# Cross-attention and quantised FFN on one core: SyncE's loads reordered and grouped, the exponential ahead of the rounding, one small POOL move at the end

## Chip, cores and metric

One Trainium2 chip, one core. The metric is the device time of one launch in microseconds, the median of several runs. Inputs and outputs are float32 in HBM (the FFN weights are int8).

## What is computed

```python
x = x + xattn(layernorm(x), ctx, ctx, W, bias, mask)      # x, ctx: 8 x 512 x 512, mask: 8 x 512 x 512
x = x + ffn(layernorm(x), weight_q, weight_scale, ffn_bias)

def xattn(q1, key, value, weights, bias, drop_mask):
    scores = einsum('bqd,bkd->bqk', q1, key) / 0.72
    attn = softmax(scores, axis=-1) * drop_mask
    o = einsum('bqk,bkd->bqd', attn, value) + bias
    return einsum('bqd,de->bqe', o, weights)

def ffn(x, weight_q, weight_scale, bias):
    x_scale = maximum(max(abs(x), axis=-1), 1e-6) / 127.0
    x_q = clip(round(x / x_scale), -128, 127)               # int8
    return (x_q @ weight_q.T) * x_scale * weight_scale + bias
```

## The kernel before

The 8 x 512 rows of `x` are 32 tiles of 128 rows, four to a batch. A step `d` works on several tiles at once, and each engine runs the same sequence of steps: four first steps (tiles 0 to 3), three passes of a loop of eight steps (tiles 4 to 27, `base` 4, 12 and 20, written out by Python), and the last steps (`TAIL`, tiles 28 to 31 and what is left). All engines have their order written out by hand and meet at semaphores.

In a step `d` of the loop:

- TensorE (PE) makes `scores(d)` (12 products), `attend(d - 2)` (12, into `ps_attn`), `feed_forward(d - 4)` (4) and `next_vw(d + 4)` (12: a context tile times the attention weights). `scores` and the others in float32 are sums of three products of high and low parts, so each operand is split in two by ACT (`_hi`) and DVE or POOL (`_lo`).
- VectorE (DVE) turns the next context tile (`turn_ctx(d + 4)`, `ct_raw`), finishes the factors of the quantisation (`gains(d - 3)`), finds the row maximum (`highest`, `neg_max`), turns the next rows (`turn_x(d + 1)`, `xt_raw`), multiplies by the mask (`masked`, `probs(d)`), adds the residual (`residual(d - 2)`, `x`), turns the probabilities that came back from DRAM (`turn_probs(d - 1)`, `pt_raw`, L1223), and makes the low parts, `pt_lo` last.
- ScalarE (ACT) does `split_next_ctx` (`ct_hi`, L878), `round_integers(d - 3)` (`x_round`, L958), `store_integers(d - 3)` (`x_int`, L970), `exponentials` (L981), `split_next_x` (`xt_hi`, L913), `add_up_x(d + 4)` (the row sum of `x_in`, L896, for the layernorm), `split_late_vw`, `centre`, `split_bounced_probs(d - 1)` (`pt_hi`, L1000), `add_up_x1_squares` (`ps_ct`, L1017), `add_up_squares`, `normalise(d + 3)`, and then issues two DMAs of its own: the store of the normalised rows, and the store of a finished output tile, for which it waits for POOL's `add_up(d - 4)`.
- GpSimd (POOL) makes the low parts `ct_lo` and `xt_lo`, adds the bias, works out `rstd` by a power (`inverse_deviation`, L1569 and L1572) when ACT's squares are there, and adds up the output (`out_tile`, L1526).
- SyncE (SP) computes nothing: it waits and issues DMAs, in the order of its `step`. The queue moves on only when a wait is over and a DMA is issued.

Two things are turned by way of DRAM. The normalised rows are stored by ACT and read back by SP in four DMAs, one for each block of 32 columns (`load_rows`, L488). The probabilities are stored by SP (`store_probs(d - 1)`, L526), and when the store has landed SP reads them back in four DMAs (`load_probs(d - 1)`, L535) into `p_blocks`, which lies in `wq_rows`. `turn_integers(d - 4)` (L543) is a DMA transpose of `x_int`.

SP's step before, in order: context pair (only when `d` is even: four DMAs, L479), `turn_integers(d - 4)`, `load_rows(d + 1)`, `store_probs(d - 1)`, `load_x(d + 4)` (L470), `load_mask(d + 2)` (L492), `load_probs(d - 1)`. `x_in` has eight places for tiles, `mask_in` four, `ctx_in` four. `add_up_x(d + 4)` of ACT's step `d` is the first to read the tile that SP loads in its own step `d`.

## Time and profile before

| | |
|---|---|
| time, median of 3 runs | 329.21 us (328.72 to 329.78) |
| the profiled execution's own time | 328.42 us |
| its span | 326.6 us |
| TensorE busy, granted clock | 311.9 us (95%), 0.998 |
| DVE, ACT, POOL busy | 261.0 us (80%), 240.6 us (74%), 259.3 us (79%) |
| DMA | 68.39 MB, 209 GB/s over the span |
| chain that ended last, by engine | SPq 24%, DMA 22%, POOL 15%, ACT 11%, issue 9%, PE 9%, DVE 7% |

The busy time of TensorE counts matmuls whose ends are modelled, and they overlap: one of 512 columns is shown with 0.39 us, and the next starts 0.23 us later. So a busy share near 100% says only that it seldom stood still, and the pace is read from starts. "SPq" and "ACTq" are the issuing of DMAs by SyncE and ScalarE. A time in brackets at the end of a row is how long the engine had been idle before it, and for whom.

### The profile page before, as it was taken

What the parts mean: (1) busy time and instruction counts of PE and PEld (TensorE: products, weight loads), DVE (VectorE), ACT (ScalarE), POOL (GpSimd) and SP (SyncE); (2) the same over time, 40 slices, a digit from 0 to 9 for tenths busy, and PEclk for the clock granted to TensorE, in tenths of its full rate; (3) what the DMA queues carried; (4) which work ended last, traced back from release to release, by engine and by line L of the source; (5) the groups of instructions that cost most, each with busy time, mean ns of one, the idle gap of its engine ahead of it and who ended that gap; (6) DMA issues with size and microseconds to landing.
All of it is one profiled execution on the core that took longest, in us unless ns stands there. A gap on an engine that the chain in (4) does not pass through costs nothing.

```text
span 326.6 us, 5339 instructions
## 1 busy us (share of the span) xinstructions
PE 311.9 (95%) x1418; PEld 239.5 (73%) x1418; DVE 261.0 (80%) x565; ACT 240.6 (74%) x494; POOL 259.3 (79%) x362
## 2 busy tenths in 40 slices
PE   8999989999999999899998999999999999999982
PEld 7888767777777678677776777767778676776671
DVE  2998765988886899688887888788888778879775
ACT  5467867887887788788876889788787878866440
POOL 3274587897999789799997989899898879858683
PEclk9999999999999999999999999999999999999999
DMA  7995985798968979997888969998897996451112
GB/s 215 264 228 186 200 216 192 220 219 249 247 202 261 238 228 194 271 229 232 259 243 228 265 200 238 243 251 237 244 243 201 234 241 192 147 159 49 50 63 98
DMA packets 88173, 68.39 MB, mean 209 GB/s; under 512 B 25040, under 2 KB 67792, under 8 KB 88144
## 3 DMA queue, kind: packets, MB, share of 16 engines
q1 hardware_dynamic: 80368, 53.90, 65.3%
q10 hardware_dynamic: 7776, 14.16, 12.0%
q8 instruction: 11, 0.18, 0.3%
q14 instruction: 18, 0.15, 0.2%
HBM read 41.16 MB, written 22.54 MB: 195 GB/s over the span
## 4 chain that ended last, share of the span: by engine, by line
SPq 24%; DMA 22%; POOL 15%; ACT 11%; issue 9%; PE 9%; DVE 7%; ACTq 1%; POOLq 0%; DVEq 0%
DMA prob_rows<-probs 10%; DMA wq_rows<-prob_rows 8%; SPq L488 8%; SPq L535 7%; POOL out_tile L1526 5%; SPq L543 5%; SPq L479 4%; ACT x_round L958 2%; ACT ps_ct L1017 2%; POOL rstd L1572 2%; DVE pt_raw L1223 2%; ACT ct_hi L878 2%; ACT x_int L970 2%; POOL x_in L1560 2%; DMA norm_rows<-x_norm 1%
## 5 line engine op out<-in xcount | busy, mean ns | idle before, releaser
L636 PE MATMUL ps_attn<-vw_hi,pt_hi 128*128 128x512 f32 x120 | 47.9, 399 | 3.6 <-DVE pt_lo L1123 3.6
L636 PE MATMUL ps_scores<-ct_hi,xt_hi 128*128 128x512 f32 x124 | 48.7, 393 | 1.1 <-POOL xt_lo L1541 1.0
L638 PE MATMUL ps_scores<-ct_hi,xt_lo 128*128 128x512 f32 x124 | 48.3, 389 | 0.0
L637 PE MATMUL ps_scores<-ct_lo,xt_hi 128*128 128x512 f32 x124 | 48.3, 389 | 0.0
L638 PE MATMUL ps_attn<-vw_hi,pt_lo 128*128 128x512 f32 x120 | 46.8, 390 | 0.0
L637 PE MATMUL ps_attn<-vw_lo,pt_hi 128*128 128x512 f32 x120 | 46.8, 390 | 0.0
L1248 DVE TENSOR_TENSOR probs<-ps_scores,mask_in 128x512 f32<-128x512 f32 x32 | 22.0, 687 | 26.7 <-ACT ps_scores L981 26.3
L878 ACT ACTIVATE ct_hi<-ct_raw 128x512 fp32r<-128x512 f32 x28 | 17.7, 632 | 33.1 <-POOL out_tile L1526 30.4
L1560 POOL TENSOR_TENSOR x_in<-x_in,bias_w 128x512 f32<-128x512 f32 x32 | 41.5, 1296 | 0.7 <-issue 0.7
L1541 POOL TENSOR_TENSOR xt_lo<-xt_raw,xt_hi 128x512 fp32r<-128x512 f32 x29 | 37.7, 1301 | 4.1 <-ACT xt_hi L913 4.1
L1526 POOL TENSOR_TENSOR out_tile<-ffn_out,x_plus 128x512 f32<-128x512 f32 x28 | 39.6, 1415 | 0.0
L1586 POOL TENSOR_TENSOR x_plus<-x,ffn_bias_wide 128x512 f32<-128x512 f32 x28 | 36.3, 1297 | 3.7
L1533 POOL TENSOR_TENSOR ct_lo<-ct_raw,ct_hi 128x512 fp32r<-128x512 f32 x28 | 36.7, 1309 | 2.8 <-ACT ct_hi L878 2.8
L1139 DVE STREAM_TRANSPOSE xt_raw<-x_blocks 128x512 f32<-128x512 f32 x30 | 33.1, 1103 | 1.1 <-DMA x_blocks<-norm_rows 1.1
L810 PE MATMUL ps_ffn<-wq_t,xq_t 128*128 128x512 bf16 x120 | 31.1, 382 | 0.8 <-ACT xq_t L952 0.7
L1139 DVE STREAM_TRANSPOSE ct_raw<-ctx_in 128x512 f32<-128x512 f32 x28 | 30.8, 1099 | 0.0
L636 PEld LDWEIGHTS ps_attn<-vw_hi,pt_hi 128*128 128x128 f32 x120 | 22.5, 188 | 11.0 <-DVE pt_lo L1123 6.5
L888 ACT ACTIVATE x_norm<-x_in,norm 128x512 f32<-128x512 f32 x32 | 25.7, 804 | 5.2 <-POOL norm L1508 5.2
L636 PEld LDWEIGHTS ps_scores<-ct_hi,xt_hi 128*128 128x128 f32 x124 | 23.3, 188 | 7.1 <-POOL xt_lo L1541 2.4
L958 ACT ACTIVATE x_round<-x_neg,round_magic,neg_gain 128x512 f32<-128x512 f32 x31 | 24.9, 803 | 3.7 <-DVE neg_gain L1277 3.7
L636 PE MATMUL ps_vw<-w_hi,ct_hi 128*128 128x512 f32 x64 | 27.3, 427 | 0.0
L638 PEld LDWEIGHTS ps_scores<-ct_hi,xt_lo 128*128 128x128 f32 x124 | 23.3, 188 | 4.9
(187 smaller groups left out, 820.8 us busy)
## 6 DMA issues: line engine op xcount, KB each, us to landing
x_in<-in_x_dram SPq DMA_DIRECT2D x32, 256.0 KB, 4.1
mask_in<-in_mask_BxSxS_fk_dram SPq DMA_DIRECT2D x32, 256.0 KB, 4.4
norm_rows<-x_norm ACTq DMA_DIRECT2D x30, 256.0 KB, 4.0
x_blocks<-norm_rows SPq DMA_DIRECT2D x120, 64.0 KB, 2.4
ctx_in<-in_ctx_dram SPq DMA_DIRECT2D x56, 128.0 KB, 3.9
prob_rows<-probs SPq DMA_DIRECT2D x24, 256.0 KB, 2.3
wq_rows<-prob_rows SPq DMA_DIRECT2D x96, 64.0 KB, 3.5
out_dram<-out_tile ACTq DMA_DIRECT2D x24, 256.0 KB, 4.3
```

The costliest lines, as they stand in the source:

```text
L488: sp.dma_start(blocks.rearrange("i (a c) -> i a c", a=QUADS), quads[:, :, b * P:(b + 1) * P]).then_inc(x_blocks_loaded[slot(n, 2)], 16)
L636: nc.tensor.matmul(bank_, lhs_hi(t), rhs_hi(t), start=(t == 0), stop=False)
L637: nc.tensor.matmul(bank_, lhs_hi(t), rhs_lo(t), start=False, stop=False)
L638: last = nc.tensor.matmul(bank_, lhs_lo(t), rhs_hi(t), start=False, stop=(t == NT - 1))
L810: last = nc.tensor.matmul(ffn_bank(base, n)[:, :], xq_t[:, slot(n, 2), t, :], wq_t[:, t, :], start=(t == 0), stop=(t == NT - 1))
L958: nc.scalar.activation(x1_round[:, slot(n, 2), :], x1_neg[:, slot(n, 2), :], ACT.Identity, bias=round_magic[:, 0:1], scale=col(neg_gain, n ...
L1139: nc.vector.transpose(into.rearrange("p t (a i) -> p t a i", a=QUADS), blocks.rearrange("p (a j t) -> p t a j", a=QUADS, t=NT)).then_inc(r ...
L1526: nc.gpsimd.tensor_tensor(out_tile[:, slot(n, 2), :], ffn_out[:, slot(n, 2), :], x1_plus_of(base, n), ALU.add).then_inc(out_ready, 1)
L1533: nc.gpsimd.tensor_tensor(ct_lo[:, batch_of(n), :, j * P:(j + 1) * P], ct_raw[:, slot(n, 2), :, :], ct_hi[:, batch_of(n), :, j * P:(j + 1) ...
L1541: nc.gpsimd.tensor_tensor(flat(xt_lo[:, slot(n, 2), :, :]), flat(xt_raw[:, slot(n, 2), :, :]), flat(xt_hi[:, slot(n, 2), :, :].bitcast(F32 ...
L1560: nc.gpsimd.tensor_tensor(x_in[:, slot(d, 8), :], x_in[:, slot(d, 8), :], bias_w[:, :], ALU.add).then_inc(x_plus_ready, 1)
L1586: nc.gpsimd.tensor_tensor(into, x1_of(base, n), ffn_bias_wide[:, :], ALU.add).then_inc(x1_plus_ready, 1)
```

## The change

It has four parts.

1. SP's step becomes: `turn_integers(d - 4)`, `store_probs(d - 1)`, `load_rows(d + 1)`, `load_probs(d - 1)`, then what is loaded ahead. The store and the reading back of the probabilities move ahead of the rows and of `x` and the mask.
2. `x` and mask are loaded two tiles by one DMA, in even steps only (`load_two`), and the waits on their semaphores are rewritten for it (`wait_x`, `wait_mask`). The context pair is loaded at the end of two steps instead of at the start of one: one block in the even step, three in the odd one (`load_half_pair`).
3. In ACT's middle steps `exponentials` moves ahead of `round_integers` and `store_integers`.
4. For the last tile POOL's `inverse_deviation` moves ahead of `add_ffn_bias(d - 2)` and `add_up(d - 4)`.

```diff
--- before.py
+++ after.py
@@ -134,6 +134,22 @@
     ring = len(sems)
     uses = (PHASE + n) // ring + 1
     eng.wait_ge(sems[slot(n, ring)], base * (16 // ring) + (16 * uses - PHASE * (16 // ring)))
+
+
+def wait_x(eng, sems, tile):
+
+    if tile < PER_BATCH:
+        eng.wait_ge(sems[tile], 16)
+    else:
+        eng.wait_ge(sems[(tile - tile % 2) % 8], 16 * (tile // 8 + 1))
+
+
+def wait_mask(eng, sems, tile):
+
+    if tile < 2:
+        eng.wait_ge(sems[tile], 16)
+    else:
+        eng.wait_ge(sems[(tile - tile % 2) % 4], 16 * (tile // 4 + 1))
 
 
 def wait_pair(eng, sems, base, n):
@@ -479,6 +495,17 @@
                     sp.dma_start(blocks.rearrange("i t (a c) -> i (t a) c", a=QUADS),
                                  rows[:, :, b * P:(b + 1) * P]).then_inc(loaded[k // 2], 16)
 
+            def load_half_pair(base, n, h):
+
+
+                wait_count(sp, ct_raw_ready, base, n - 4 + 2 - PER_BATCH)
+                k = slot(n, 4)
+                rows = ctx_flat[bass.ds((base + n) * P, 2 * P), :].rearrange("(a i) d -> i a d", i=BLOCK)
+                for b in range(h, 1 if h == 0 else QUADS):
+                    blocks = ctx_in[b * BLOCK:(b + 1) * BLOCK, k:k + 2, :]
+                    sp.dma_start(blocks.rearrange("i t (a c) -> i (t a) c", a=QUADS),
+                                 rows[:, :, b * P:(b + 1) * P]).then_inc(ctx_loaded[k // 2], 16)
+
             def load_rows(base, n, row):
 
                 quads = norm_rows[bass.ds(row, P), :].rearrange("(a i) d -> i a d", i=BLOCK)
@@ -487,6 +514,11 @@
                     blocks = x_blocks[b * BLOCK:(b + 1) * BLOCK, slot(n, 4), :]
                     sp.dma_start(blocks.rearrange("i (a c) -> i a c", a=QUADS),
                                  quads[:, :, b * P:(b + 1) * P]).then_inc(x_blocks_loaded[slot(n, 2)], 16)
+
+            def load_two(into, rows, row, k, loaded):
+
+                sp.dma_start(into[:, k:k + 2, :], rows[bass.ds(row, 2 * P), :].rearrange("(t p) d -> p t d", p=P)) \
+                    .then_inc(loaded[k], 16)
 
             def load_mask(tile, k):
                 sp.dma_start(mask_in[:, k, :], mask_rows[bass.ds(tile, P), :]).then_inc(mask_loaded[k], 16)
@@ -551,15 +583,11 @@
             def step(base, d, row):
 
                 bounced = in_loop(base)
-                n = d + 4
-                if n % 2 == 0 and exists(base, n) and not is_tile(base, n, PER_BATCH) \
-                        and not is_tile(base, n, PER_BATCH + 2):
-
-                    wait_count(sp, ct_raw_ready, base, n - 4 + 2 - PER_BATCH)
-                    load_blocks(ctx_in, ctx_flat, row + n * P, n, 2, ctx_loaded)
                 n = d - 4
                 if exists(base, n) and (in_loop(base) or base + n < BY_PE):
                     turn_integers(base, n)
+                if bounced:
+                    store_probs(base, d - 1, row + (d - 1) * P)
                 n = d + 1
                 if is_tile(base, n, BY_PE_ROWS):
 
@@ -568,17 +596,17 @@
                 if exists(base, n) and not is_tile(base, n, 1) and (not last_batch(base) or d == 0):
                     load_rows(base, n, row + n * P)
                 if bounced:
-                    store_probs(base, d - 1, row + (d - 1) * P)
+                    load_probs(base, d - 1, row + (d - 1) * P)
                 n = d + 4
-                if exists(base, n):
-
-                    wait_count(sp, x1_ready, base, n - 8 + 1)
-                    load_x(row + n * P, slot(n, 8))
+                if exists(base, n) and d % 2 == 0:
+
+                    wait_count(sp, x1_ready, base, n + 1 - 8 + 1)
+                    load_two(x_in, x_rows, row + n * P, slot(n, 8), x_loaded)
                 n = d + 2
-                if exists(base, n):
-
-                    wait_count(sp, probs_ready, base, n - 4 + 1)
-                    load_mask(row + n * P, slot(n, 4))
+                if exists(base, n) and d % 2 == 0:
+
+                    wait_count(sp, probs_ready, base, n + 1 - 4 + 1)
+                    load_two(mask_in, mask_rows, row + n * P, slot(n, 4), mask_loaded)
                 if is_tile(base, d, 1):
                     load_ffn_constants()
                     sp.wait_ge(wq_rows_ready, 1)
@@ -588,8 +616,10 @@
                 if is_tile(base, d, PER_BATCH - 1):
 
                     sp.wait_ge(wq_turned, 16 * NT)
-                if bounced:
-                    load_probs(base, d - 1, row + (d - 1) * P)
+
+                n = d + 6 - d % 2
+                if exists(base, n) and base + n >= 2 * PER_BATCH:
+                    load_half_pair(base, n, d % 2)
                 n = d - 5
                 if is_tile(base, n + 1, LAST):
                     store_out(base, n, row + n * P)
@@ -890,7 +920,7 @@
 
             def add_up_x(base, n):
 
-                wait_dma(act, x_loaded, base, n)
+                wait_x(act, x_loaded, base + n)
                 if is_tile(base, n, SUMS_FROM):
                     act.wait_ge(xt_lo_ready, BY_PE_ROWS)
                 nc.scalar.activation(ps_xt[:, :], x_in[:, slot(n, 8), :], ACT.Identity,
@@ -1019,10 +1049,10 @@
 
                 if is_middle(base, d):
                     split_next_ctx(d + 4)
+                    exponentials()
                     if in_loop(base):
                         round_integers(d - 3)
                         store_integers(d - 3)
-                    exponentials()
                     split_next_x()
                     add_up_x(base, d + 4)
                     if in_loop(base):
@@ -1161,7 +1191,7 @@
 
             def x_statistics(base, n):
 
-                wait_dma(dve, x_loaded, base, n)
+                wait_x(dve, x_loaded, base + n)
                 nc.vector.bn_stats(stats1[:, slot(n, 4), :], x_in[:, slot(n, 8), :]).then_inc(stats1_ready, 1)
                 wait_count(dve, stats1_ready, base, n + 1)
 
@@ -1239,7 +1269,7 @@
                 def masked():
 
                     wait_count(dve, exp_ready, base, d + 1)
-                    wait_dma(dve, mask_loaded, base, d)
+                    wait_mask(dve, mask_loaded, base + d)
                     into, exps, mask_tile = probs[:, slot(d, 2), :], ps_scores[:, :], mask_in[:, slot(d, 4), :]
                     if is_middle(base, d) and base + d < TAIL - 1:
                         into = into.rearrange("p (b t j) -> p t b j", b=QUADS, t=NT)
@@ -1552,7 +1582,7 @@
 
                 def add_bias():
 
-                    wait_dma(pool, x_loaded, base, d)
+                    wait_x(pool, x_loaded, base + d)
                     if is_tile(base, d, 0):
                         pool.wait_ge(bias_w_ready, 1)
 
@@ -1636,10 +1666,10 @@
                         add_up(d - 4)
                         add_ffn_bias(d - 2)
                     else:
+                        if is_tile(base, d - 1, LAST):
+                            inverse_deviation(d - 1)
                         add_ffn_bias(d - 2)
                         add_up(d - 4)
-                    if is_tile(base, d - 1, LAST):
-                        inverse_deviation(d - 1)
                     if is_tile(base, d - 1, LAST):
                         add_ffn_bias(d - 1)
                 if is_tile(base, d - 2, LAST):
```

What the SP queue holds in an odd and an even step of the loop (`x_blocks` are the normalised rows, `prob_rows` the stored probabilities, `wq_rows` the place into which they are read back). Before, an even step:

```order
L479 DMA ctx_in<-in_ctx_dram 32x8x128 x4
L543 DMA_TRANSPOSE xq_t<-x_int 128x4x128
L488 DMA x_blocks<-norm_rows 32x4x128 x4
L526 DMA prob_rows<-probs 128x512
L470 DMA x_in<-in_x_dram 128x512
L492 DMA mask_in<-in_mask_BxSxS_fk_dram 128x512
L535 DMA wq_rows<-prob_rows 32x4x128 x4
```

The odd step had the same rows without the first. Now, the last row of an odd step and then an even step:

```order
L506 DMA ctx_in<-in_ctx_dram 32x8x128 x3
L575 DMA_TRANSPOSE xq_t<-x_int 128x4x128
L558 DMA prob_rows<-probs 128x512
L515 DMA x_blocks<-norm_rows 32x4x128 x4
L567 DMA wq_rows<-prob_rows 32x4x128 x4
L520 DMA x_in<-in_x_dram 128x2x512
L520 DMA mask_in<-in_mask_BxSxS_fk_dram 128x2x512
L506 DMA ctx_in<-in_ctx_dram 32x8x128
```

The odd step now begins with the same four rows and ends with the three context loads. The even step had 16 DMAs and the odd one 12; now each has 13, and `x` and the mask have moved from ahead of `load_probs` to behind it.

ACT in a step of the loop, from the split of the context tile to the sum of `x`. Before:

```order
L878 ACTIVATE ct_hi<-ct_raw 128x4x128
L958 ACTIVATE x_round<-x_neg,round_magic,neg_gain 128x512
L970 ACTIVATE x_int<-x_round 128x512
L981 ACTIVATE ps_scores,prob_sum<-ps_scores,neg_max 128x512
L913 ACTIVATE xt_hi<-xt_raw 128x512
L896 ACTIVATE ps_xt,x_sum<-x_in 128x512
```

Now:

```order
L908 ACTIVATE ct_hi<-ct_raw 128x4x128
L1011 ACTIVATE ps_scores,prob_sum<-ps_scores,neg_max 128x512
L988 ACTIVATE x_round<-x_neg,round_magic,neg_gain 128x512
L1000 ACTIVATE x_int<-x_round 128x512
L943 ACTIVATE xt_hi<-xt_raw 128x512
L926 ACTIVATE ps_xt,x_sum<-x_in 128x512
```

The exponential is two places earlier; `x_int` is one place later, and the sum of `x` stays where it was.

## Rows read from the trace of the kernel before

**Rows 1.** Timeline, TensorE: first product of scores for tiles 4, 8, 9, 28, and a pause

```profile
51.74 0.50 PE L636 MATMUL ps_scores<-ct_hi,xt_hi 128*128 128x512 f32 x1
...
88.21 0.39 PE L636 MATMUL ps_scores<-ct_hi,xt_hi 128*128 128x512 f32 x1
...
97.29 0.39 PE L636 MATMUL ps_scores<-ct_hi,xt_hi 128*128 128x512 f32 x1
...
213.71 0.50 PE L636 MATMUL ps_attn<-vw_hi,pt_hi 128*128 128x512 f32 x1 [0.56 <-DVE pt_lo L1123]
...
277.15 0.39 PE L636 MATMUL ps_scores<-ct_hi,xt_hi 128*128 128x512 f32 x1
```

**Rows 2.** Waits: engine, line, waited for: us in total, times, longest

```profile
ACT ct_hi L878 <- POOL out_tile L1526: 30.4, 23, 1.4
DVE probs L1248 <- ACT ps_scores L981: 26.3, 27, 1.3
...
DVE pt_raw L1223 <- DMA wq_rows<-prob_rows: 10.5, 11, 1.7
```

**Rows 3.** Timeline, SP's queue in an even step (start, us, what)

```profile
199.08 1.19 SPq L543 DMA_TRANSPOSE xq_t<-x_int  x1
200.32 2.00 SPq L488 DMA_DIRECT2D x_blocks<-norm_rows  x4
202.36 0.43 SPq L526 DMA_DIRECT2D prob_rows<-probs  x1
202.84 0.43 SPq L470 DMA_DIRECT2D x_in<-in_x_dram  x1
...
205.04 2.06 SPq L535 DMA_DIRECT2D wq_rows<-prob_rows  x4
```

**Rows 4.** Timeline, ACT: two steps without a pause, then the step from 205.10

```profile
91.62 0.63 ACT L878 ACTIVATE ct_hi<-ct_raw 128x512 fp32r<-128x512 f32 x1 [1.31 <-POOL out_tile L1526]
...
100.56 0.63 ACT L878 ACTIVATE ct_hi<-ct_raw 128x512 fp32r<-128x512 f32 x1 [1.32 <-POOL out_tile L1526]
...
204.71 0.34 ACTq L1039 DMA_DIRECT2D out_dram<-out_tile  x1
205.10 0.63 ACT L878 ACTIVATE ct_hi<-ct_raw 128x512 fp32r<-128x512 f32 x1 [1.32 <-POOL out_tile L1526]
...
206.47 0.63 ACT L970 ACTIVATE x_int<-x_round 128x512 bf16<-128x512 f32 x1
207.01 0.64 ACT L981 ACTIVATE ps_scores<-ps_scores,neg_max 128x512 f32<-128x512 f32 x1
...
208.19 0.59 ACT L896 ACTIVATE ps_xt<-x_in 128x512 f32<-128x512 f32 x1
```

**Rows 5.** DMA issues of the span: x count, KB, median us to landing

```profile
x_in<-in_x_dram SPq DMA_DIRECT2D x32, 256.0 KB, 4.1
mask_in<-in_mask_BxSxS_fk_dram SPq DMA_DIRECT2D x32, 256.0 KB, 4.4
```

**Rows 6.** DMA issues at 193.48 (first row) and at 166.27 (second row)

```profile
mask_in<-in_mask_BxSxS_fk_dram SPq DMA_DIRECT2D x1, 256.0 KB, 3.0
...
mask_in<-in_mask_BxSxS_fk_dram SPq DMA_DIRECT2D x1, 256.0 KB, 5.6
```

**Rows 7.** Timeline, DVE: probabilities of tile 3

```profile
49.58 0.65 DVE L1248 TENSOR_TENSOR probs<-ps_scores,mask_in 128x512 f32<-128x512 f32 x1
```

**Rows 8.** Timeline, POOL and DVE at the end, from the last tile's mean

```profile
314.42 0.21 DVE L1304 BATCH_NORM_AGGREGATE meanvar<-last_stats 128x2 f32<-128x12 f32 x1
...
314.42 1.27 POOL L1586 TENSOR_TENSOR ctx_in<-x,ffn_bias_wide 128x512 f32<-128x512 f32 x1
...
315.42 0.69 DVE L1262 TENSOR_REDUCE abs_max<-x_neg 128x1 f32<-128x512 f32 x1 [0.25 <-ACT x_neg L1011]
...
317.15 0.55 POOL L1572 TENSOR_TENSOR rstd<-var_eps,minus_half 128x1 f32<-128x1 f32 x1
...
317.81 0.21 DVE L1269 TENSOR_SCALAR q_range<-abs_max,rstd 128x1 f32<-128x1 f32 x1 [1.70 <-POOL rstd L1572]
```

## Prediction

> **What bounds the kernel now.** I read the page first. TensorE is shown busy for 95% of the span (the table above), so the question is how far it is from its own pace. The timeline of TensorE gives that: from the first scores product of tile 8 to that of tile 9 it is 97.29 - 88.21 = 9.08 us, with nothing idle between. The 24 steps of the loop run from 51.74 to 277.15 [rows 1], 225.4 us; 24 at 9.08 would be 217.9. So the loop has **7.5 us** of pauses to give, and no more. One of them is the row at 213.71, where the product with the probabilities waited for `pt_lo` [rows 1].
>
> The waits say why. DVE sat 10.5 us in eleven waits, up to 1.7 us, for the probabilities to come back from DRAM (`wq_rows<-prob_rows`), and `pt_lo` is made from these [rows 2]. SP's queue shows why they are late: in an even step it issues a transpose, four row loads, the store, `x` and the mask, and only then, at 205.04, four loads of probabilities, 5.96 us after the step's first issue [rows 3]. A context pair of over 2 us more stands ahead of all that.
>
> A second cycle lies right under TensorE's. ACT waits 30.4 us in all for POOL's `out_tile` before `ct_hi` [rows 2], and `out_tile` waits for ACT's squares through `rstd`: squares, `rstd`, `out_tile`, the store on ACT's queue, `ct_hi`, and along ACT back to the squares. Where nothing disturbs it, `ct_hi` follows `ct_hi` after 100.56 - 91.62 = 8.94 us [rows 4]. Two steps make 17.88 us against TensorE's 18.16. So ACT has **0.28 us for two steps** to lose, and whatever it waits beyond that lengthens the loop as if TensorE waited.
>
> **The change part by part.** The sum is made against the profiled execution's own 328.42 us; the median of the runs is 0.79 us above it.
>
> (a) *Probabilities earlier.* I count from ACT's `ct_hi` of step d. `x_int` ends at 206.47 + 0.63 - 205.10 = 2.00, and the exponential that is now ahead of it adds 0.66 (0.64 and the gap): 2.66, and SP issues the transpose at about 2.72. From the starts there [rows 3]: transpose 1.24, store 0.48, row loads 2.04. The loads of the probabilities begin at 6.5; the store, issued at 3.96, has then had 2.5 us (its wait before, with x and mask issued behind it, ended at 205.04 - 202.36 = 2.7). The last is issued at about 8.1 and DVE needs them about 12 after the same `ct_hi`: its own next step is 8.94 on, and maximum, turn, mask and residual, some 3 us, lie ahead of `turn_probs` in it. The eleven waits should go: **-7.5 us**. Above nothing, at worst 0, if they are late for the transpose ahead of the store.
>
> (b) *Exponential first.* DVE's 26.3 us of waiting for it [rows 2] shrink, about 1 us a step. DVE isn't the bound, so by itself this is worth 0; it is cover for (a). Its price is that `x_int`, on which SP's step now hangs first, is 0.66 later. TensorE uses the integers a step later, behind 24 products of 0.23 us: 0.
>
> (c) *x in pairs, behind the probabilities.* This is the new wait. The loads of the probabilities take about 1.9 (2.06 in [rows 3]), so the pair is issued at 8.4. Its first tile is summed in the very next ACT step, at 208.19 - 205.10 = 3.09 after `ct_hi` [rows 4], which is 8.94 + 3.09 = 12.03. It may take **3.65 us** to land, and 3.93 before the 0.28 is used up. What it will take no row shows, since no DMA before was of 512 KB. Nearest rows: one tile of `x` takes 4.1 median, and the mask issued 0.47 behind it lands after 4.4 [rows 5], so 512 KB in two DMAs are there 4.9 after the first issue. Lower end: the mask at 193.48 with 3.0 + 0.47 = 3.5; upper end: the one at 166.27 with 5.6 + 0.47 = 6.1 [rows 6]. I take **4.4**, between 4.1 and 4.9, because in those rows a 256 KB store stood directly ahead, and now small loads do, but ACT's store of an output tile, which it issues 0.39 ahead of `ct_hi` [rows 4], so at 8.55 on this count, falls on the same moment, with the store of the rows just ahead of it. Twelve even steps load a pair: 12 x (4.4 - 3.93) = **+5.6 us**. Ends: 0 at 3.5, and +26 at 6.1 if that were every step, which no stretch of the trace supports. Behind the waiting sum on ACT stand `vw_hi`, `x_neg`, `pt_hi` and the squares, so POOL's `rstd`, `out_tile` and `ct_lo` wait with it, and TensorE for `ct_lo`.
>
> [...]
>
> (d) *First even step of the loop.* Here SP is held by the store of tile 3's probabilities, ready at 49.58 + 0.65 = 50.2 [rows 7], not by `x_int`. The pair goes out 0.48 + 2.04 + 1.9 later, at 54.7, about 1 us later against its reader than in the other steps: **+1.0** (0 to 2).
>
> (e) *Context in parts.* The same four DMAs in two pieces; the last is issued about 10 after `ct_hi` of one step and used at about 16: 0. Masks are used two steps later: 0. Two issues fewer in two steps: SP is no longer the bound, 0. The first steps: fewer issues ahead of the rows and later probabilities, 0 (from -0.5 to +0.5).
>
> (f) *rstd of the last tile.* The last mean is there at 314.42 + 0.21 = 314.63; POOL then runs 2.5 us of additions, and DVE waits 1.70 us until 317.81 for `rstd` [rows 8]. Now POOL can begin at 314.7 and be done at 315.5; next late is `abs_max`, at 315.42 + 0.69 = 316.1. So `q_range` moves from 317.81 to 316.2, and all behind it to the last store: **-1.6 us**. The additions moved behind it feed stores that are not last: 0. The lower end is 0.5 if ACT's or TensorE's work on the last two tiles becomes the next wait.
>
> Sum: -7.5 + 5.6 + 1.0 - 1.6 = -2.5, so 325.9 for the profiled execution and **326.7 us** for the median. About 1 us, 0.3%, is what a measurement of this kernel can tell from no change.
>
> **The rivals.**
>
> *The pair is in time.* If it lands within 3.9 us, (c) is nothing and (d) about 0.3: -7.5 + 0.3 - 1.6 = -8.8, which is 320.4 us. For it speak the row with 3.0 us [rows 6] and that no large store is directly ahead; against it the median of 4.1 for half as much.
>
> *The pair is later, and the kernel slower.* The place is ACT's sum of `x` in even steps. It gives back the gain from 12 x (L - 3.93) = 8.1 on, that is from a landing time of L = 4.6. With L = 5.0 it is 12 x 1.07 = 12.8 against 8.1: +4.7, or 333.9 us. For it speak 4.9 for two DMAs of the same bytes, and ACT's two stores at the moment of the pair; against it that the store ahead is gone. [...]
>
> *The probabilities are no earlier in effect.* The store now directly follows the transpose, SP's step hangs on a later `x_int`, and the pauses stay, with no wait for `x` that matters. Then only (f) is left: 327.6 us. Against it: about 4 us between the last issue and the need.
>
> **How the numbers follow.** The forecast has 0.45, the pair in time 0.2, the pair later 0.25, no earlier 0.1. The range takes the pair in time at its low end, 320.4, and at its high end L = 4.9: 12 x 0.97 = 11.6 against 8.1, +3.5, so 332.7; I give 320.5 to 332.5. The forecast's own range, L from 4.2 to 4.6, is 324 to 329. Faster by over 0.3%: 0.34 of the forecast, 0.2, and 0.06 of the last: 0.6. Within 0.3%: 0.06, 0.04 of the later pair and 0.04: 0.14. Slower: 0.05 and 0.21: 0.26.
>
> **What would show it.** The wait of `pt_raw` for `wq_rows` gone from DVE, and DVE's wait for the exponential well under 26.3 us. A new wait of ACT's sum of `x` (`ps_xt`) for `x_in`, in about twelve even steps, of 0.5 to 1 us each, with a pair landing at 4.4. Even steps of TensorE longer than odd ones, two together 18.4 to 18.7. At the end DVE waits for `abs_max`'s input and not for `rstd`. I am wrong if the sum of `x` doesn't wait, if `pt_raw` still does, or if `xt_raw` waits for its rows, which are issued about 0.6 later than before.

## The result, and the profile after

The changed kernel takes 342.72 us (median of 4 runs, 340.27 to 347.44) against 329.50 for the kernel before on the same chip: a ratio of **1.0375** (95% interval 1.0264 to 1.0486). It is slower by 3.7%, where 326.7 us were forecast, and outside the range of 320.5 to 332.5. The profiled execution is the longest of the four and counts as a slow one, 347.44 us with a span of 345.6, so a second profile of the same kernel, nearer its usual time, follows in the experiments, and sizes are given from both.

**Where it went.** The timeline of TensorE after (start, us, what), first scores product of tiles 4, 12, 13, 14 and 28:

```profile
50.96 0.50 PE L666 MATMUL ps_scores<-ct_hi,xt_hi 128*128 128x512 f32 x1 [0.16 <-POOL xt_lo L1571]
...
132.17 0.39 PE L666 MATMUL ps_scores<-ct_hi,xt_hi 128*128 128x512 f32 x1
...
141.25 0.39 PE L666 MATMUL ps_scores<-ct_hi,xt_hi 128*128 128x512 f32 x1
...
152.95 0.39 PE L666 MATMUL ps_scores<-ct_hi,xt_hi 128*128 128x512 f32 x1
...
295.88 0.39 PE L666 MATMUL ps_scores<-ct_hi,xt_hi 128*128 128x512 f32 x1
```

One step takes the undisturbed 9.08 us, the next 11.70, and so on in turn; over the loop the long ones take 10.1 to 13.3. The 24 steps take 295.88 - 50.96 = 244.9 us, where they took 225.4 [rows 1] and could take 217.9. The stretch ahead of them (50.96 against 51.74) and the one behind (295.88 to the span's end, 49.7, against 49.5) are as before: all 19 us are in the loop.

The waits after (engine, line, waited for: us in total, times, longest):

```profile
DVE vw_lo L1153 <- ACT vw_hi L948: 41.8, 24, 4.1
ACT ct_hi L908 <- POOL out_tile L1556: 35.1, 23, 1.6
ACT ps_xt L926 <- DMA x_in<-in_x_dram: 28.5, 12, 3.4
...
PE ps_attn L666 <- DVE pt_lo L1153: 13.0, 11, 2.3
...
DVE probs L1278 <- ACT ps_scores L1011: 7.0, 24, 1.3
...
DVE pt_raw L1253 <- DMA wq_rows<-prob_rows: 3.4, 5, 1.2
```

Two of the waits of before [rows 2] have shrunk as forecast, `pt_raw`'s from 10.5 to 3.4 us and `probs`' from 26.3 to 7.0. A new one stands in their place: ACT's sum of `x`, twelve times, 2.4 us on average. What stands behind the sum on ACT waits with it: `vw_hi`, on which DVE's longest wait is, and through `pt_hi` and `pt_lo` TensorE. Its place in a step, in ACT's timeline and SP's (start, us, what):

```profile
135.98 0.63 ACT L908 ACTIVATE ct_hi<-ct_raw 128x512 fp32r<-128x512 f32 x1 [1.53 <-POOL out_tile L1556]
...
138.55 0.62 ACT L943 ACTIVATE xt_hi<-xt_raw 128x512 fp32r<-128x512 f32 x1
141.86 0.60 ACT L926 ACTIVATE ps_xt<-x_in 128x512 f32<-128x512 f32 x1 [2.69 <-DMA x_in<-in_x_dram]
```

```profile
130.99 0.57 SPq L558 DMA_DIRECT2D prob_rows<-probs  x1
...
135.42 3.01 SPq L520 DMA_DIRECT2D x_in<-in_x_dram  x1
138.47 0.47 SPq L520 DMA_DIRECT2D mask_in<-in_mask_BxSxS_fk_dram  x1
```

The sum belongs at about 3.1 behind `ct_hi` [rows 4], and starts at 5.88. The store of the probabilities went out 3.98 after the `ct_hi` at 127.01, and the pair of `x` 8.41 after it; the median of the loop's issues is 8.4. (Its issue took 3.01 us here and 2.20 in one other step, and 0.43 to 0.48 in the other ten.) The page's DMA issues after:

```profile
mask_in<-in_mask_BxSxS_fk_dram SPq DMA_DIRECT2D x15, 512.0 KB, 6.9
...
x_in<-in_x_dram SPq DMA_DIRECT2D x14, 512.0 KB, 6.2
```

One tile had landed after 4.1 and a mask after 4.4 [rows 5]; the pair takes 6.2.

The end of the program after, DVE and POOL, from the last tile's mean:

```profile
333.42 0.21 DVE L1334 BATCH_NORM_AGGREGATE meanvar<-last_stats 128x2 f32<-128x12 f32 x1
...
333.98 0.55 POOL L1602 TENSOR_TENSOR rstd<-var_eps,minus_half 128x1 f32<-128x1 f32 x1
...
335.14 0.21 DVE L1299 TENSOR_SCALAR q_range<-abs_max,rstd 128x1 f32<-128x1 f32 x1
...
335.73 1.26 POOL L1556 TENSOR_TENSOR out_tile<-ffn_out,ctx_in 128x512 f32<-128x512 f32 x1
335.84 1.31 DVE L1342 TENSOR_SCALAR x_round<-x_neg,neg_gain 128x256 f32<-128x256 f32 x1
336.96 1.30 POOL L1616 TENSOR_TENSOR ct_raw<-ctx_in,ffn_bias_wide 128x512 f32<-128x512 f32 x1
337.18 1.24 DVE L1348 TENSOR_SCALAR x_int<-x_round 128x256 bf16<-128x256 f32 x1
```

`q_range` stands 1.72 behind the mean and no longer 3.39 [rows 8]: the 1.6 us are there. But POOL's additions, two of which had run ahead of `rstd`, now run beside DVE's rounding. The same two DVE instructions in the timeline of the kernel before:

```profile
318.50 0.57 DVE L1312 TENSOR_SCALAR x_round<-x_neg,neg_gain 128x256 f32<-128x256 f32 x1
319.11 0.29 DVE L1318 TENSOR_SCALAR x_int<-x_round 128x256 bf16<-128x256 f32 x1
```

After, each of the two ends 0.16 us behind the POOL addition beside it (337.15 and 336.99, 338.42 and 338.26), and together they take 2.55 us where they took 0.86 (in which the first, too, ends 0.14 behind an addition of POOL's, that from 317.67 to 318.93). From the first scores product of tile 31 to the span's end it is 24.7 us in both kernels. So step (f) gave nothing at the end of the program, and these rows show where its 1.6 us went.

### The profile page after: what moved, and what is told of

Same layout as the page of the kernel before. It is cut to its first block, busy times and chain, and to the rows that moved or that the text cites. A ratio compares the mean times of both kernels' runs of the same rounds, so it can differ in the third digit from the quotient of the medians.

```text
span 345.6 us, 5295 instructions
## 1 busy us (share of the span) xinstructions
PE 316.8 (92%) x1403; PEld 242.3 (70%) x1418; DVE 265.6 (77%) x565; ACT 237.8 (69%) x494; POOL 264.6 (77%) x362
## 4 chain that ended last, share of the span: by engine, by line
DMA 26%; SPq 19%; ACT 19%; POOL 13%; issue 8%; PE 7%; DVE 6%; ACTq 1%; POOLq 0%; DVEq 0%
DMA x_in<-in_x_dram 21%; SPq L515 7%; SPq L567 6%; POOL out_tile L1556 6%; SPq L575 4%; POOL rstd L1602 4%; ACT x_round L988 3%; ACT ps_scores L1011 3%; ACT ps_ct L1047 3%; ACT ct_hi L908 3%; ACT x_neg L1041 3%; ACT x_int L1000 2%; ACT vw_hi L948 2%; SPq L558 2%; DMA norm_rows<-x_norm 2%
## 5 line engine op out<-in xcount | busy, mean ns | idle before, releaser
L666 PE MATMUL ps_attn<-vw_hi,pt_hi 128*128 128x512 f32 x120 | 50.0, 417 | 13.1 <-DVE pt_lo L1153 13.0
L667 PE MATMUL ps_attn<-vw_lo,pt_hi 128*128 128x512 f32 x120 | 48.0, 400 | 0.0
L668 PE MATMUL ps_attn<-vw_hi,pt_lo 128*128 128x512 f32 x120 | 47.8, 398 | 0.0
L666 PEld LDWEIGHTS ps_attn<-vw_hi,pt_hi 128*128 128x128 f32 x120 | 23.3, 194 | 22.7 <-DVE pt_lo L1153 18.1
L1556 POOL TENSOR_TENSOR out_tile<-ffn_out,x_plus 128x512 f32<-128x512 f32 x28 | 36.1, 1288 | 0.0
L1153 DVE TENSOR_TENSOR vw_lo<-ps_ut,vw_hi 128x512 fp32r<-128x512 f32 x14 | 9.7, 691 | 34.0 <-ACT vw_hi L948 34.0
L926 ACT ACTIVATE ps_xt<-x_in 128x512 f32<-128x512 f32 x27 | 16.0, 592 | 28.5 <-DMA x_in<-in_x_dram 28.5
L840 PE MATMUL ps_ffn<-wq_t,xq_t 128*128 128x512 bf16 x105 | 27.7, 380 | 1.9 <-ACT xq_t L982 0.9
L666 PE MATMUL ps_ut<-w_hi,ct_hi 128*128 128x512 f32 x56 | 23.4, 419 | 5.1 <-POOL ct_lo L1563 4.4
L1602 POOL TENSOR_TENSOR rstd<-var_eps,minus_half 128x1 f32<-128x1 f32 x32 | 26.1, 817 | 2.5
L666 PEld LDWEIGHTS ps_scores<-ct_hi,xt_hi 128*128 128x128 f32 x124 | 23.3, 188 | 6.4 <-POOL xt_lo L1571 1.6
```

Source lines behind the costliest of these rows:

```text
L666: nc.tensor.matmul(bank_, lhs_hi(t), rhs_hi(t), start=(t == 0), stop=False)
L667: nc.tensor.matmul(bank_, lhs_hi(t), rhs_lo(t), start=False, stop=False)
L668: last = nc.tensor.matmul(bank_, lhs_lo(t), rhs_hi(t), start=False, stop=(t == NT - 1))
L840: last = nc.tensor.matmul(ffn_bank(base, n)[:, :], xq_t[:, slot(n, 2), t, :], wq_t[:, t, :], start=(t == 0), stop=(t == NT - 1))
L1556: nc.gpsimd.tensor_tensor(out_tile[:, slot(n, 2), :], ffn_out[:, slot(n, 2), :], x1_plus_of(base, n), ALU.add).then_inc(out_ready, 1)
L1602: nc.gpsimd.tensor_tensor(col(rstd2, n), col(var_eps2, n), minus_half[:, :], ALU.pow).then_inc(rstd2_ready, 1)
```

## The experiments

Ratios are against the kernel before on the same chip, with their 95% intervals; it took 327.5 to 329.4 us there. "Loop" is the time from the first scores product of tile 4 to that of tile 28; without a pause it is 217.9.

**x one tile a DMA, at its new place.**

```diff
-                if exists(base, n) and d % 2 == 0:
-                    wait_count(sp, x1_ready, base, n + 1 - 8 + 1)
-                    load_two(x_in, x_rows, row + n * P, slot(n, 8), x_loaded)
+                if exists(base, n):
+                    wait_count(sp, x1_ready, base, n - 8 + 1)
+                    load_x(row + n * P, slot(n, 8))
```

The three waits of `wait_x` go back to `wait_dma` with it.

> The changed kernel, but x is again loaded one tile at a time in every step, at its new place behind the loads of the probabilities; masks stay in pairs. Theory 'size' (the pair of 512 KB lands after 6.2 us, one tile would after 4.1): ACT's sum of x waits 8.4 + 4.1 - 12.0 = 0.5 us, now in all 24 steps, the loop has 24 x 9.5 = 227 us instead of 245 and the kernel about 327 us. Theory 'place' (behind the probabilities and beside ACT's two stores anything lands late): landing stays at 5.5 to 6 us, the sum waits about 2 us in every step, and the kernel is slower than the change, 355 us or more.

336.98 us, ratio 1.0257 (1.0220 to 1.0293), loop 231.8. ACT waits 12.9 us in 19 steps for a tile that lands after 4.4. That is close to the wait of theory 'size' (24 times 0.5), and 'place' is refuted; but the loop and the time of 'size', 227 and 327 us, were both too low: 217.9 and a wait of 12 us are 230 already. Smaller loads help by a third of the loss; at this place even one tile is late.

**The pair right behind the store of the probabilities.**

```diff
                 if bounced:
                     store_probs(base, d - 1, row + (d - 1) * P)
+                n = d + 4
+                if exists(base, n) and d % 2 == 0:
+                    wait_count(sp, x1_ready, base, n + 1 - 8 + 1)
+                    load_two(x_in, x_rows, row + n * P, slot(n, 8), x_loaded)
```

It is taken out of its place behind `load_probs`.

> The changed kernel, but the pair of x is issued right behind the store of the probabilities, 4.5 us after ct_hi instead of 8.4; everything else as in the change. If the late pair is the cause, it may take 7.5 us to land and takes about 6.2: no wait of ACT's sum, steps of 9.1 us, the loop near 218 to 220 us and the kernel 322 to 325 us. If the context in parts, the masks in pairs or the exponential's place cost the time, it stays near 340 us.

323.98 us, ratio **0.9872** (0.9817 to 0.9928), loop 219.5. The waits of this kernel, in which ACT's for `x_in` is gone:

```profile
ACT ct_hi L908 <- POOL out_tile L1556: 34.2, 23, 1.7
DVE xt_raw L1169 <- DMA x_blocks<-norm_rows: 15.1, 15, 2.1
...
DVE pt_raw L1253 <- DMA wq_rows<-prob_rows: 9.3, 12, 2.6
```

Its page's row of the load:

```profile
x_in<-in_x_dram SPq DMA_DIRECT2D x14, 512.0 KB, 4.1
```

The same 512 KB land after 4.1 us, and are issued 4.7 behind `ct_hi` instead of 8.4. So the place of one statement turns the change from slower into faster, and a pair that is issued early is in time.

**Only POOL's move at the end, in the kernel before.**

```diff
                     else:
+                        if is_tile(base, d - 1, LAST):
+                            inverse_deviation(d - 1)
                         add_ffn_bias(d - 2)
                         add_up(d - 4)
-                    if is_tile(base, d - 1, LAST):
-                        inverse_deviation(d - 1)
```

> The kernel before with POOL's move for the last tile alone. Prediction step (f): 1.6 us less. [...]

327.93 us, ratio 0.9963 (0.9921 to 1.0005): no gain that can be told from none. Step (f) had 1.6 us; the estimate for this run, made from the 1.31 and 1.24 us that the two DVE instructions take in the changed kernel, was the time of before within 0.3 us. The timeline of its end:

```profile
315.78 1.27 POOL L1526 TENSOR_TENSOR out_tile<-ffn_out,ctx_in 128x512 f32<-128x512 f32 x1
315.89 1.31 DVE L1312 TENSOR_SCALAR x_round<-x_neg,neg_gain 128x256 f32<-128x256 f32 x1
317.01 1.31 POOL L1586 TENSOR_TENSOR ct_raw<-ctx_in,ffn_bias_wide 128x512 f32<-128x512 f32 x1
317.24 1.23 DVE L1318 TENSOR_SCALAR x_int<-x_round 128x256 bf16<-128x256 f32 x1
```

Alone, the move meets the same collision.

**Only the exponential first, in the kernel before.**

```diff
+                    exponentials()
                     if in_loop(base):
                         round_integers(d - 3)
                         store_integers(d - 3)
-                    exponentials()
```

> The kernel before with the exponential ahead of the rounding alone. Prediction step (b): DVE's wait for the exponential falls from 26 us to about 7, the probabilities are ready about 1 us sooner, but SP is busy then and stores them no sooner, x_int is 0.66 later: no change within 1 us. Rival: the transpose at the head of SP's step starts 0.66 later in the odd steps and the loads of the probabilities of the even steps come later with it: 1 to 4 us slower.

333.56 us, ratio 1.0155 (1.0104 to 1.0207), loop 229.4. Two of its waits:

```profile
DVE pt_raw L1223 <- DMA wq_rows<-prob_rows: 36.9, 22, 3.1
```

```profile
SPq L541 <- ACT x_int L970: 18.7, 16, 2.3
```

SP's wait for `x_int` was 9.5 us before, and `pt_raw`'s 10.5 [rows 2]. SP's step hangs on `x_int`; with `x_int` 0.65 later, everything on that queue is later, and the loads of the probabilities stand last in it. (b) was costed at nothing, and in the kernel before it costs 4 us of loop and 5.3 us of time, more than the 1 to 4 that the rival had.

**x one tile a DMA, early.** The edit of the first kernel, at the place of the second.

> The change with x loaded one tile a DMA again, but right behind the store of the probabilities (masks stay in pairs). Theory A, the place decides: like the pair at this place, x lands after about 4.1 us and is there in time, the loop takes about 219.5 us and the time is within 1.5 us of the 324.0 of that kernel. Rival, the size decides (a pair at the early place saves an issue and a wait of SP in every second step): two issues more in two steps delay the rows by 0.4 us a step, and the time is 326 us or more.

321.04 us, ratio **0.9763** (0.9697 to 0.9830), loop 218.9. It is 2.9 us below the 324.0, where 1.5 was allowed, but only 0.6 of that is in the loop. The rest is in the ramp: the loop starts at 50.6 here and at 52.7 there, and this start moves by itself (50.4 to 54.8 over all profiles, in pairs and in singles alike).

**ACT's output store cut to 16 of 128 rows.**

```diff
-   act.dma_start(out_rows[bass.ds((base + n) * P, P), :], out_tile[:, slot(n, 2), :])
+   act.dma_start(out_rows[bass.ds((base + n) * P, 16), :], out_tile[0:16, slot(n, 2), :])
```

> The change with ACT's store of the output tile cut to 16 of its 128 rows in the middle steps; it leaves most of the output unwritten. Theory A, the pair is late because ACT's stores share the queues' engines with it at that moment: the pair lands after 4.1 to 4.6 us instead of 6.2, ACT's wait for x_in (28.5 us) falls below 8, and the time is 322 to 328 us. Rival B, the pair's own size and the mask pair directly behind it set the landing: it stays at 5.9 to 6.3 us and the time at 340 to 344.

335.80 us, ratio 1.0152 (1.0051 to 1.0252), loop 231.0. The pair lands after 4.6, at the upper end of what was expected, but ACT still waits 13.5 us, and the time is of neither theory: the store can be a part of the lateness at most, not all of it. Run again:

> The change with ACT's output store cut to 16 of 128 rows in the middle steps, a second time (it leaves most of the output unwritten). If the store is what holds the pair up, it lands after 4.3 to 4.8 us again and the time is 334 to 337 us; if its first landing of 4.6 was within what profiles of one kernel differ by, it lands after 5.0 or more and the time is 338 or more.

336.57 us, ratio 1.0282 (1.0218 to 1.0346), loop 232.8, landing 4.8, wait 16.8. So the shorter landing comes back, at the upper end of what was expected for it.

**Mask pairs in odd steps.**

```diff
-                n = d + 2
-                if exists(base, n) and d % 2 == 0:
-                    wait_count(sp, probs_ready, base, n + 1 - 4 + 1)
-                    load_two(mask_in, mask_rows, row + n * P, slot(n, 4), mask_loaded)
...
+                n = d + 3
+                if exists(base, n) and d % 2 == 1:
+                    wait_count(sp, probs_ready, base, n + 1 - 4 + 1)
+                    load_two(mask_in, mask_rows, row + n * P, slot(n, 4), mask_loaded)
```

(Only the first of these pairs stays in step 0.)

> The change with the mask pairs loaded in odd steps, so that no 512 KB stands directly behind the x pair. Theory B, the pair and the mask pair share the engines and each delays the other: x lands after 4.2 to 4.8 us instead of 6.2, ACT's wait for x_in falls from 28.5 us to 10 or less, and the time is 325 to 332 us. Rival A, ACT's stores cause the lateness: x stays at 5.9 to 6.3 us and the time at 340 to 344.

349.51 us, ratio 1.0608 (1.0537 to 1.0679), loop 244.8: slower than the change. Both theories missed it. `x` lands after 5.3, but is issued 9.0 behind `ct_hi` and not 8.4. At its new place the mask pair must wait for the probabilities of the step's own tile (SP stands 44.5 us for them, in thirteen waits) and so goes out within about 2 us of the next step's store of the probabilities. That store then lands after 3.0 us and not 2.3 in the even steps, the reading back begins at 7.2 and not 6.5, and `x` stands behind it on SP's queue. That it is the mask pair in flight which slows the store fits, but isn't shown by itself. The wait of 28.5 us is unchanged.

**Both at once.** The output store cut and the mask pairs in odd steps.

> The change with both edits: ACT's output store cut to 16 of 128 rows in the middle steps (it leaves most of the output unwritten) and the mask pairs loaded in odd steps. Theory, the two neighbours together make the pair late: each alone took 1.6 and 0.9 us off its landing of 6.2, both together bring it to 3.7 to 4.2 us, as at the early place, ACT waits less than 8 us for it, and the loop is 219 to 226 us. Rival, the late place itself is slow (context blocks, other loads): it stays at 4.6 or above.

342.58 us, ratio 1.0466 (1.0375 to 1.0558), loop 237.3. The landing is 4.3, close to the 4.1 of the early place, and still ACT waits 21.2 us, because the issue is at 9.2. The expected 219 to 226 us of loop had left that out.

**The change again.**

> The change itself, unchanged, for a second profile. Theory, each even step is longer by what ACT waits for x: loop minus 217.9 equals ACT's wait for x_in within 3 us, as in the five late kernels so far, with a pair landing at 5.8 to 6.3, 340 to 344 us. Rival, the first profile was a bad run: the landing is below 5.2 and the loop has pauses that no wait for x explains.

339.47 us, ratio 1.0385 (1.0326 to 1.0444), the first ratio again. Its loop is 236.0, so 18.1 above 217.9. Its wait (from the waits), and its load (from the page's DMA issues):

```profile
ACT ps_xt L926 <- DMA x_in<-in_x_dram: 20.1, 13, 2.9
```

```profile
x_in<-in_x_dram SPq DMA_DIRECT2D x14, 512.0 KB, 5.2
```

The landing was expected at 5.8 or more; it is 5.2, and 6.2 in the first profile. One profile of a landing is good to about 1 us here.

**The late pair, exponential behind the rounding again.** The change with the edit of the fourth kernel taken back.

> The change with the exponential back behind the rounding and everything else as it is. Theory, twelve even steps are each as long as x is late: the exponential first puts SP's transpose, and with it the pair, about 0.55 us later, so without it the pair is issued 7.85 us after ct_hi instead of 8.4, the landing stays near 6.2 us, ACT waits about 22 us for it instead of 28.5, and the time is 6 us less: 334 to 338 us. Rival, the lateness is made of something that doesn't move with the issue (a transfer on another queue that ends at its own time): 341 to 344 us.

340.44 us, ratio 1.0324 (1.0255 to 1.0392), loop 234.9. The store of the probabilities is 0.55 sooner (3.42), the pair is issued at 7.9, and it lands after 5.7: at 13.6, just when it did in the second profile of the change (8.4 + 5.2). It was to gain 6 us, and gained 2 at most by the ratios. Half a microsecond at the issue is less than what two profiles of one kernel differ by at the landing, so whether it brings the pair sooner can't be seen here.

The late kernels together, and the early pair beside them; all times are medians from one profile each. The issue counts from `ct_hi` of the step before the reader's, "arrival" is issue plus landing, and the sum of `x` is due at 12.0.

| kernel | issued | landing | arrival | ACT's wait for x | loop - 217.9 |
|---|---|---|---|---|---|
| the change, first profile | 8.4 | 6.2 | 14.6 | 28.5 | 27.0 |
| second profile | 8.4 | 5.2 | 13.6 | 20.1 | 18.1 |
| exponential behind | 7.9 | 5.7 | 13.6 | 19.4 | 17.0 |
| masks in odd steps | 9.0 | 5.3 | 14.3 | 28.5 | 26.9 |
| store cut | 8.4 | 4.6 | 13.0 | 13.5 | 13.1 |
| store cut, again | 8.4 | 4.8 | 13.2 | 16.8 | 14.9 |
| both | 9.2 | 4.3 | 13.5 | 21.2 | 19.4 |
| pair early | 4.7 | 4.1 | 8.8 | none | 1.6 |

Two things can be read from it. What ACT waits for `x` is what the loop is longer by, to within 2.4 us: the wait is all that these kernels lose against a loop without a pause. And the three landings with ACT's store cut (4.3, 4.6, 4.8) all lie below the four without the cut (5.2, 5.3, 5.7, 6.2): 1.0 us with the masks in odd steps, 0.4 to 1.6 with them behind `x`, of which the upper end rests on the longest execution alone. Moving the mask pair takes off nothing that stands clear of the spread (5.3 against 5.2 and 6.2). So ACT's output store, which in these kernels goes out within 1 us of the pair in most steps, is a part of the landing, some 0.4 to 1.0 us. What is left above the 4.1 of the early place, 0.2 to 0.7 us, the spread could cover, and it wasn't taken apart: ACT's other store, of the normalised rows and also of 256 KB, goes out 0.1 to 2 us ahead of the late pair and 2 to 3.5 us behind the early one, and no run leaves it out.

**Early pair, exponential behind.**

> The change with the x pair right behind the store (324.0 us), and the exponential back behind the rounding. Theory, the exponential first has the price that it had alone in the kernel before (333.6 against 328.3, through the integers that SP's step hangs on): without it the time is 320 to 322.5 us, with less waiting of pt_raw for wq_rows than the 9.3 us. Rival, with the probabilities' loads sooner the later integers cost nothing and the earlier exponential gives cover: 324 to 326 us.

322.06 us, ratio **0.9798** (0.9735 to 0.9860), loop 218.05. Two rows of TensorE's timeline, tiles 4 and 28:

```profile
52.38 0.50 PE L666 MATMUL ps_scores<-ct_hi,xt_hi 128*128 128x512 f32 x1
...
270.43 0.39 PE L666 MATMUL ps_scores<-ct_hi,xt_hi 128*128 128x512 f32 x1
```

Nothing is left to gain in this loop: it has all of the 7.5 us, and `pt_raw` waits once, 1.2 us, where the kernel with the exponential first had 9.3. Even with the early pair the exponential first costs something, 1.4 us of loop against the pair with the exponential first.

**Early single x, exponential behind; then with the tail's rounding in PSUM; then with single masks.** The second keeps the last tile's centred rows in a PSUM bank that is free by then:

```diff
+        def x1_neg_of(base, n):
+            return ps_vw[:, :] if is_tile(base, n, LAST) else x1_neg[:, slot(n, 2), :]
...
-   nc.vector.tensor_scalar(x1_round[:, slot(n, 2), half_of(h)], x1_neg[:, slot(n, 2), half_of(h)],
+   nc.vector.tensor_scalar(ps_vw[:, half_of(h)], ps_vw[:, half_of(h)],
```

> The change with x one tile a DMA right behind the store of the probabilities (321.0 us) and the exponential back behind the rounding. Theory, the two gains come from different waits: the first gave a start of the loop at 50.6 us (52.7 with pairs), the second a loop of 24 x 9.08 = 218 us without a pause (218.9 there): 319.5 to 320.7 us, ratio 0.971 to 0.976. Rival, the earlier exponential was cover that single loads need: the waits of pt_raw come back and the time is 322 us or more.

> The kernel before it in this list, with the last tile's centred rows and its rounding kept in a PSUM bank that is free then. [...]

> The first kernel of this list with the masks too one tile a DMA (only the context loads stay in parts). Theory, pairs of masks are worth nothing, since SP has slack and no row waits for them: within 0.8 us of the first kernel. Rival, the 256 KB mask in every step delays the loads behind it, and the time is 1 us or more longer.

The first: 321.10 us, ratio 0.9759 (0.9720 to 0.9797), loop 218.06. The loop is as expected and the time 0.4 us above its range; that single loads start it sooner is not so, for its sister starts at 53.1 with them. With single masks: 321.25 us, 0.9767 (0.9716 to 0.9817), the same. With the PSUM tail: 320.42 us, **0.9738** (0.9701 to 0.9775), the lowest of all ratios, though its interval overlaps the first's and the step between them, 0.002, is half of the 0.004 that the author's estimate had at least; it also had 0.3 to 0.5 us for each of the two DVE instructions, and an end 1.2 to 1.9 us sooner. The trace is plainer than the times: from the first scores product of tile 31 to the span's end it is 23.3 us, and 24.7 in the first. Its end:

```profile
311.09 1.27 POOL L1560 TENSOR_TENSOR out_tile<-ffn_out,ctx_in 128x512 f32<-128x512 f32 x1
311.18 0.49 DVE L1346 TENSOR_SCALAR ps_vw<-ps_vw,neg_gain 128x256 f32<-128x256 f32 x1
311.70 0.42 DVE L1352 TENSOR_SCALAR x_int<-ps_vw 128x256 bf16<-128x256 f32 x1
```

DVE rounds in 0.49 us in the middle of POOL's 1.27. From PSUM they are longer than undisturbed ones from SBUF (0.35 and 0.29), but they don't wait. This shows what the 2.55 us depend on: with the source out of SBUF the two take 0.91 us together and not 2.55, with POOL's addition beside them, and the end comes 1.4 us sooner. Why POOL's addition holds up the two from SBUF isn't shown.

**One statement moved: the loads of the probabilities ahead of the mask.**

```diff
                     load_x(row + n * P, slot(n, 8))
+                if bounced:
+                    load_probs(base, d - 1, row + (d - 1) * P)
                 n = d + 2
```

They are taken out of their place behind the mask.

> The kernel before with one statement moved: the loads of the probabilities ahead of the mask's load. Theory, step (a) needs no more than this: x is issued where it was and no large load stands ahead of the probabilities but x, so pt_raw's wait of 10.5 us falls below 3, the loop takes 218 to 220 us instead of 225.4, and the time is 321 to 324 us (ratio 0.974 to 0.986). Rival, the probabilities' store still ends too late, because the row loads and x stand beside it: pt_raw waits 7 us or more and the time is 326 us or more.

335.92 us, ratio 1.0276 (1.0212 to 1.0341), loop 234.6 (50.68 to 285.27), and `pt_raw` waits 17.1 us: the rival, in both of its signs. SP's wait for the store, and one step of its queue:

```profile
SPq L535 <- DMA prob_rows<-probs: 45.7, 24, 3.7
```

```profile
147.92 0.43 SPq L526 DMA_DIRECT2D prob_rows<-probs  x1
148.39 0.43 SPq L470 DMA_DIRECT2D x_in<-in_x_dram  x1
150.94 1.80 SPq L535 DMA_DIRECT2D wq_rows<-prob_rows  x4
152.79 0.43 SPq L492 DMA_DIRECT2D mask_in<-in_mask_BxSxS_fk_dram  x1
```

From 148.82 to 150.94 SP stands for the store to land, 45.7 us in all (23.4 before), with the mask's issue no longer in that gap. Its own step becomes the bound: for `x_int`, on which the step's first issue hangs, it waits only 2.5 us in all (9.5 before), and in the chain that ended last SP's issuing has 37% (24% before). `x` goes out at 8.0 and not 6.3, the store at 7.5 and not 5.8. Moved ahead of the mask's load, the loads of the probabilities came later, not sooner: the first is issued 10.4 us after `ct_hi` in the median, and 8.4 in the kernel before.

**The order alone: transpose, store, x, rows, probabilities, mask.**

> The kernel before with SP's step in the order transpose, store of the probabilities, x, row loads, loads of the probabilities, mask; every load as before (context pairs of four in one step, x and mask one tile each, rounding ahead of the exponential, rstd late). Theory, the order alone makes the gain: the row loads cover the store's landing, the probabilities are asked for at about 6.3 us after ct_hi, the loop is 218 to 219.5 us and the time 320.5 to 323.5 (ratio 0.975 to 0.985). Rival, SP has no room: with the context pair of over 2 us in one step it still falls behind as in the kernel with one statement moved, pt_raw waits over 7 us, and the time is 325 or more.

320.23 us, ratio **0.9791** (0.9736 to 0.9846). The same stretch of SP's queue:

```profile
147.02 0.47 SPq L526 DMA_DIRECT2D prob_rows<-probs  x1
147.54 0.43 SPq L470 DMA_DIRECT2D x_in<-in_x_dram  x1
148.01 1.87 SPq L488 DMA_DIRECT2D x_blocks<-norm_rows  x4
149.93 0.43 SPq L535 DMA_DIRECT2D wq_rows<-prob_rows  x1
```

The row loads' 1.87 us fill the time that the store takes, and SP goes on without a gap. The wait is 10.2 us in all, the loop 268.60 - 50.54 = 218.06, without pairs, context in parts or an earlier exponential. The order gives the whole gain, as expected; only the reading back begins later than the 6.3 us of the expectation, at 7.0 in the median.

## Why the prediction was wrong

**What bounds the kernel**: right. The loop had 7.5 us to give, and five kernels came down to 218.05 or 218.06, against 217.9 without a pause.

**(a) Probabilities earlier, -7.5**: right in mechanism and size. The store went out at 3.98 (3.96 forecast) and the waits shrank; its cause is SP's order, in which the rows' issue covers the store's landing. The change could not show the gain.

**(b) Exponential first, 0**: wrong by itself, +4 us of loop in the kernel before and 1.4 with the early pair. The price that the step names, "`x_int`, on which SP's step now hangs first, is 0.66 later", is the right one; but it was set against TensorE's need of the integers alone, and not against what is queued behind the transpose on SP.

**(c) The pair, +5.6**: this is the step that failed, by the size of one term. Issue at 8.4, the due time, the place of the wait and twelve steps of it are all as forecast. "I take **4.4**" was the error: it lands after 5.2 in one profile and 6.2 in the other. From the landings, 12 x (5.2 - 3.93) is 15.2 and 12 x (6.2 - 3.93) is 27.2, against 18.1 and 27.0 measured. The step had named ACT's output store as falling on the same moment, and took 4.4 all the same; the kernels that store 16 of its 128 rows show 0.4 to 1.0 us for it. What it forecast behind the sum came too, except that TensorE waits more for `pt_lo` (13.0 us) than for the `ct_lo` that it named (4.4). The upper end, 6.1, which "no stretch of the trace supports" for every step, is what one profile shows for the median step. The range was closed at a landing of 4.9 and so left out the ends that the step itself had set.

**(d) First even step, +1.0**: its step takes 10.50 us after, no longer than the even steps behind it; the first pair goes out 8.45 behind `ct_hi`, like the others, so this delay did not come. **(e)**: 0, as forecast; masks one or two a DMA differ by 0.15 us, and with the whole context pair in one step the loop is the same 218.06.

**(f) rstd, -1.6**: `q_range` came 1.6 sooner, and the end not at all. "The additions moved behind it feed stores that are not last: 0" looked at who reads their results and not at what runs beside them. The kernel with the source in PSUM gets 1.4 us of it.

Of the rivals it was *the pair is later, and the kernel slower*, decided from a landing of 4.6 on as worked out there. It was given 0.25 and 333.9 us, at a landing of 5.0. Its own sum with a landing of 6.2 gives 27.2 - 7.5 = +19.7 for the loop, where the first profile shows 244.9 - 225.4 = +19.5; with 5.2 it gives +7.7, where the second shows +10.6. The medians of the time are 12 to 13 us above those of the kernel before. The formula takes the median landing for every step, and the second profile's slower steps, from 9.9 to 11.9 us, show how far that is from each.

## What to carry to other kernels

A load's place in a queue decides by two numbers: first by when it is issued (3.7 us later here), and then by how long it takes to land there, here 1 to 2 us more, of which ACT's output store beside it had 0.4 to 1.0; where the slack is 0.3 us in two steps, its landing time has to be bounded by the worst of the rows and not by their middle. A queue that must wait for one of its own stores should have something to issue in that time: with the row loads and `x` between store and read-back the kernel here took 2.1% less, and with `x` alone between them 2.8% more. Work that is moved out of the way of a critical instruction on one engine may land beside the next critical one on another, as here, where two DVE instructions took 2.55 us beside POOL's additions and 0.86 before: check what runs beside it as well as who reads it.

## What the runs showed of the hardware

- The same 512 KB load lands after 4.1 us at one place in the step and after 5.2 and 6.2 at another, 3.7 us later, in two profiles; one of 256 KB after 3.2 to 4.0 (early, in five kernels) and 4.4 (late). Without most of a 256 KB store beside it, the late one takes 4.3 to 4.8.
- Two DVE `tensor_scalar` of 128x256 from SBUF take 1.31 and 1.24 us beside POOL's additions of 1.26 to 1.30, ending 0.16 behind each, and 0.35 and 0.29 alone. With their source in PSUM they take 0.49 and 0.42 beside POOL's additions.
- A pair's issue on SP took 3.01 and 2.20 us in two of twelve steps, and 0.43 to 0.48 otherwise; 1.86 and 1.71 in the second profile, and up to 1.69 for single tiles at the same place. Why isn't shown.
